# A recurrence phase on one core: tile scores as sums over rows, scores turned by transposes over two banks, fewer keys in a block's first half

## The reference, cut to what matters

```python
def step(state, inp):                       # 8 heads of 64, for each position
    k_t, v_t, w_t, r_t = inp
    kv = k_t[..., :, None] * v_t[..., None, :]
    state = (1.0 - w_t)[..., :, None] * state + kv
    out = jnp.einsum('bhd,bhde->bhe', r_t, state)
    return (state, out)
...
y = outs.transpose(1, 0, 2, 3).reshape(Bv, Tv, Cv) @ Wo.T
...
slope_sign = jnp.sign(jnp.mean(spline_slopes, axis=-1))      # 64 tiles x 8 dims
tile_sigs = tile_sigs.at[jnp.arange(NUM_TILES)[:, None], DIMS].set(slope_sign)
cluster_sigs = jnp.sign(tile_sigs.reshape(NUM_CLUSTERS, TILES_PER_CLUSTER, D).mean(axis=1))
input_sigs = jnp.sign(xf)                                    # xf: the normed rows
cluster_scores = input_sigs @ cluster_sigs.T
best_cluster = jnp.argmax(cluster_scores, axis=-1)
tile_scores = input_sigs @ tile_sigs.T
in_cluster = cluster_assign[None, :] == best_cluster[:, None]
tile_idx = jnp.argmax(jnp.where(in_cluster, tile_scores, -jnp.inf), axis=-1)
```

## Time and profile before

| | |
|---|---|
| median of 3 executions | 8651.39 us (8645.66 to 8653.18) |
| the profiled execution | 8648.8 us, span 8647.0 us |
| core_phase, 7060 to 8430 us: busy PE, DVE, POOL, ACT | 1211.48, 1069.02, 671.15, 357.77 of 1370 us |
| scan_phase, 390 to 5200 us: busy PE, DVE, POOL, ACT | 4345.28, 4543.37, 4439.76, 3671.34 of 4810 us |
| granted TensorE clock, core_phase | 0.87 of full |

### The profile page before, as it was taken

One profiled execution on the slowest core, in us unless ns is written; L12 is line 12 of the kernel. 1 busy time (PEld: TensorE's weight loads), 2 busy tenths in 40 slices (PEclk: granted clock), 3 DMA queues, 4 the chain that ended last, 5 costly groups with the idle time before them and its releaser, 6 DMA issues. The chain is left out here.

```text
span 8647.0 us, 222908 instructions
## 1 busy us (share of the span) xinstructions
PE 7638.4 (88%) x76550; PEld 5615.1 (65%) x76550; DVE 6621.9 (77%) x8318; ACT 4702.7 (54%) x10584; POOL 5670.5 (66%) x3272
## 2 busy tenths in 40 slices
PE   5659999999989989989999999899999989999984
PEld 3337777777777777777777777644444436666653
DVE  4439999999999999999999999622222237878776
ACT  4447777777777777777777787511111112222220
POOL 0009999999999999999999999600000015554544
PEclk8779999999999999999999999999999988988885
DMA  3350000000000000000000000121221222222215
GB/s 134 137 158 0 20 21 0 20 21 1 19 21 20 0 21 20 0 21 20 8 13 20 20 0 5 60 83 68 87 82 68 92 79 78 76 79 74 79 66 168
DMA packets 198786, 423.53 MB, mean 49 GB/s; under 512 B 22448, under 2 KB 48496, under 8 KB 183024
## 3 DMA queue, kind: packets, MB, share of 16 engines
q1 hardware_dynamic: 172768, 382.77, 13.2%
q10 hardware_dynamic: 25872, 38.80, 1.2%
HBM read 225.11 MB, written 196.41 MB: 49 GB/s over the span
## 5 line engine op out<-in xcount | busy, mean ns | idle before, releaser
L485 POOL TENSOR_TENSOR scan_hc<-scan_h,scan_cb 128x1024 f32<-128x1024 f32 x2048 | 4776.9, 2366 | 265.8 <-DMA scan_cb<-scratch_bc 127.5
L651 DVE TENSOR_TENSOR_SCAN scan_h<-scan_a,scan_carry,scan_u 128x512 f32<-128x512 f32 x4096 | 4802.1, 1260 | 156.0 <-PE scan_u L590 128.1
L590 PE MATMUL scan_u<-scan_dg,scan_v 64*128 64x128 f32 x32768 | 2391.7, 286 | 339.1 <-DVE scan_h L651 280.1
L536 ACT ACTIVATE scan_a<-scan_dt,scan_aneg 128x512 f32<-128x512 f32 x4096 | 2659.9, 708 | 44.8 <-issue 30.5
L590 PEld LDWEIGHTS scan_u<-scan_dg,scan_v 64*128 64x128 f32 x32768 | 2000.7, 188 | 819.1 <-DVE scan_h L651 538.0
L598 PE MATMUL scan_y<-scan_ident,scan_hc 128*128 128x128 f32 x16408 | 2251.0, 280 | 60.1 <-POOL scan_hc L485 33.6
L598 PEld LDWEIGHTS scan_y<-scan_ident,scan_hc 128*128 128x128 f32 x16408 | 1764.8, 141 | 310.3 <-POOL scan_hc L485 34.5
L507 ACT ACTIVATE scan_dg<-scan_half,scan_bt 128x64 f32<-128x64 f32 x4096 | 1139.2, 341 | 5.0 <-DVE scan_onward L634 5.0
L528 ACT ACTIVATE scan_carry<-scan_h,scan_onward 128x4 f32 (+1 forms) x1008 | 303.0, 301 | 1042.5 <-DVE scan_h L651 1042.5
L177 POOL TENSOR_TENSOR mid_r<-mid_ve,mid_half_neg 128x4 f32<-128x4 f32 x32 | 32.4, 1012 | 1271.4 <-DVE mid_ve L132 784.1
L1141 POOL TENSOR_TENSOR core_joint<-core_own 128x32 f32<-128x32 f32 x64 | 17.4, 272 | 621.2 <-DVE core_own L1271 536.6
(11 more groups left out here) (211 smaller groups left out, 7647.3 us busy)
## 6 DMA issues: line engine op xcount, KB each, us to landing
scratch_y<-scan_yo ACTq DMA_DIRECT2D x17, 1024.0 KB, 4.7
pre_x<-in_x SPq DMA_DIRECT2D x16, 1024.0 KB, 6.8
scratch_z<-pre_zt SPq DMA_DIRECT2D x16, 1024.0 KB, 3.9
scratch_dt<-pre_dt SPq DMA_DIRECT2D x16, 1024.0 KB, 4.6
scratch_vr<-pre_vr ACTq DMA_DIRECT2D x16, 1024.0 KB, 4.7
scan_dt<-scratch_dt SPq DMA_DIRECT2D x16, 1024.0 KB, 5.3
scan_v<-scratch_vr SPq DMA_DIRECT2D x32, 512.0 KB, 7.8
scan_z<-scratch_z SPq DMA_DIRECT2D x16, 1024.0 KB, 10.7
```

Of the source, the lines that this page charges most:

```text
L485: pool.tensor_tensor(hc[:, q].rearrange("p n (r j) -> p n r j", j=P), h[:, q].rearrange("p n (r j) -> p n r j", j=P), cb[:, bass.ds(b * NS ...
L536: ins = act.activation(a[:, q, n, :], dt[:, par, q, :], ACT.Exp, scale=aneg[:, q, bass.ds(m * 2 + n, 1)])
L590: mm = pe.matmul(u_ps[:, q % 2, g, k * HP:(k + 1) * HP, :], v[row, par, k, q, :], dg[row, buf, k], start=True, stop=True)
L651: ins = dve.tensor_tensor_scan(h[:, q, n, :], a[:, q, n, :], u_ps[:, q % 2, :, :, n].rearrange("p g t -> p (g t)"), carry[:, q, bass.ds(m ...
```

## The change

Three things change in each item, and some constants.

1. Tile scores. `turn_x` and `tile_scores` leave PE. ACT takes the sign of `xf` directly into `sg`. POOL has a new piece, `flip`, that multiplies `sg` by a row of slope signs `sgn`, 128x512, in place. DVE's `route` then sums eight neighbours (128x512 to 128x64), sums eight of those per cluster, and combines both and `key_row` in two `scalar_tensor_tensor` instructions. `route` moves ahead of `spread_scores` in DVE's list, and `flip` stands ahead of `keys` in POOL's.
2. Turned scores. `turn_scores` becomes eight transposes of 128x128 that fill both banks of `sc_ps`; `spread_scores` reads every 16th column.
3. Products. In the first half of a block's positions only the first four keys are multiplied, 256 columns in place of 512, and ACT copies as much; the rest of `scs` is zero from a memset at the start.

The row `sgn` is made once, at the start of the phase: DVE makes four diagonals, PE multiplies them with ones, ACT copies the result; POOL, ACT and PE wait for it.

```diff
-        scores_ps = sc_ps[:, 0, 0:SUB * H].rearrange("p (t h) -> p t h", h=H)
+        turned_ps = sc_ps[:].rearrange("p g (t n) -> p (g t) n", n=P)
+        scores_ps = turned_ps[:, :, 0:P:P // H]
...
+            def flip(i, par, m):
+                act_r.wait(pool, i, 2)
+                pool_b.inc(pool.tensor_tensor(sg[:], sg[:], sgn[:], ALU.mult))
...
-            pipelined(pool, ITEMS, [(1, root), (3, totals), (4, keys), (1, pick), (4, more_keys)])
+            pipelined(pool, ITEMS, [(1, root), (3, totals), (1, flip), (4, keys), (1, pick), (4, more_keys)])
...
-                pe_r.wait(dve, i, 2)
-                dve.tensor_tensor(key[:], sc_ps[:, 1, 0:NT], key_row[:], ALU.add).then_inc(key_read, 1)
-                dve.wait_ge(key_read, i + 4)
+                pool_b.wait(dve, i, 2)
+                dve.tensor_reduce(ts[:], sg[:].rearrange("p (n e) -> p n e", e=8), AX.X, ALU.add).then_inc(key_read, 1)
+                dve.wait_ge(key_read, i + 2)
+                by_cluster = lambda t: t[:].rearrange("p (c n) -> p c n", n=8)
+                after.link(dve, dve.tensor_reduce(cl[:], by_cluster(ts), AX.X, ALU.add))
+                after.link(dve, dve.scalar_tensor_tensor(out=by_cluster(both), in0=cl[:].rearrange("p (c n) -> p c n", n=1).broadcast_to([P, NT // 8, 8]), scalar=512.0, in1=by_cluster(ts), op0=ALU.mult, op1=ALU.add))
+                after.link(dve, dve.scalar_tensor_tensor(out=key[:], in0=both[:], scalar=64.0, in1=key_row[:], op0=ALU.mult, op1=ALU.add))
...
-            pipelined(dve, ITEMS, [(1, state), (1, norms), (0, limits), (1, centred), (4, decays), (3, spread_scores), (1, route)])
+            pipelined(dve, ITEMS, [(1, state), (1, norms), (0, limits), (1, centred), (4, decays), (1, route), (3, spread_scores)])
...
+            act.wait_ge(sgn_made, 1)
+            act.copy(sgn[:], y_ps[:]).then_inc(sgn_ready, 1)
...
-                pe_r.wait(act, i, 1)
-                act_r.inc(act.activation(sgt[:], kt_ps[:], ACT.Sign))
+                after.wait(act, i, S_XF)
+                act.wait_ge(key_read, i + 1)
+                act_r.inc(act.activation(sg[:], xf[:], ACT.Sign))
...
+            for q in range(Q):
+                mm = pe.matmul(y_ps[:, q * P:(q + 1) * P], ones[:], diag[:, q, :], start=True, stop=True)
+            mm.then_inc(sgn_made, 1)
+            pe.wait_ge(sgn_ready, 1)
...
-                pe.wait_ge(key_read, i + 1)
...
-                        mm = pe.matmul(sc_ps[q * 32:(q + 1) * 32, g], heads[:].rearrange("p h n -> p (h n)"), rk[:, par, rows, :, q * NI:(q + 1) * NI].rearrange("p t j i -> p (t j) i"),
+                        mm = pe.matmul(sc_ps[q * 32:(q + 1) * 32, g, 0:SUB // 2 * seen * NI], heads[:].rearrange("p h n -> p (h n)"), rk[:, par, rows, 0:seen, q * NI:(q + 1) * NI],
...
-                    mm = pe.matmul(scores_ps[:, t, :], scs[:, t].rearrange("p i j -> p (i j)"), ident[:, 0:P:P // H], start=True, stop=True)
+                    mm = pe.transpose(turned_ps[:, t, :], scs[:, t].rearrange("p i j -> p (i j)"), ident[:])
...
-            pipelined(pe, ITEMS, [(2, tree), (2, turn_keys), (3, products), (1, turn_x), (2, reads), (3, turn_scores), (1, tile_scores), (2, sums), (2, outputs)])
+            pipelined(pe, ITEMS, [(2, tree), (2, turn_keys), (3, products), (2, reads), (3, turn_scores), (2, sums), (2, outputs)])
```

More of the change, by code:

```diff
@@ L1010, in core_phase @@
         eps_mul = sb("eps_mul", [P, 2]); eps_add = sb("eps_add", [P, 2]); keep = sb("keep", [P, 2])
-        key = sb("key", [P, NT]); kmax = sb("kmax", [P, 1]); pen = sb("pen", [P, NT]); mm2 = sb("mm2", [P, 2])
+        ts = sb("ts", [P, NT]); cl = sb("cl", [P, NT // 8]); both = sb("both", [P, NT]); key = sb("key", [P, NT]); kmax = sb("kmax", [P, 1]); pen = sb("pen", [P, NT]); mm2 = sb("mm2", [P, 2])
         oh = sb("oh", [P, ITEMS, NT]); xs = sb("xs", [P, ITEMS, 8]); ext = sb("ext", [P, 2, NT])
@@ L1043, in core_phase @@
         act_a = Count(sem("act_a"), 4)
-        after = Count(sem("after"), 15)
-        S_STATE, S_X3, S_VE, S_KEEP, S_XF, S_OH = 1, 2, 5, 10, 12, 14
-        pool_b = Count(sem("pool_b"), 2)
+        after = Count(sem("after"), 18)
+        S_STATE, S_X3, S_VE, S_KEEP, S_XF, S_OH = 1, 2, 5, 10, 12, 17
+        pool_b = Count(sem("pool_b"), 3)
         routed = Count(sem("routed"), 5)
-        pe_r = Count(sem("pe_r"), 2)
         act_r = Count(sem("act_r"), 2)
@@ L1126, in _ @@
             pool.wait_ge(pool_ready, 1)
[L1127 removed]
+            pool.wait_ge(zeroed, 11)
+            pool.wait_ge(sgn_ready, 1)
             def root(i, par, m):
@@ L1202, in _ @@
             routed.start(dve)
-            dve.sem_inc(key_read, 3)
-            for t, value in ((kz, 0.0), (rk, 0.0), (s, 0.0), (ext, -BIG), (own, 1.0), (eps_mul, 1.0), (eps_add, EPS)):
+            dve.sem_inc(key_read, 1)
+            for t, value in ((kz, 0.0), (rk, 0.0), (s, 0.0), (scs, 0.0), (ext, -BIG), (own, 1.0), (eps_mul, 1.0), (eps_add, EPS)):
                 dve.memset(t[:], value).then_inc(zeroed, 1)
@@ L1208, in _ @@
             last.then_inc(zeroed, 1)
+            dve.memset(ones[:], 1.0)
             dve.memset(rr[:, SUB - 1, SUB], 1.0).then_inc(zeroed, 1)
-            dve.wait_ge(zeroed, 9)
+            dve.wait_ge(zeroed, 10)
             dve.memset(eps_mul[:, 1:2], 1.0 + EPS)
             dve.memset(eps_add[:, 1:2], EPS * EPS).then_inc(zeroed, 1)
-            dve.wait_ge(zeroed, 10)
-            dve.wait_ge(consts, 144)
+            dve.wait_ge(zeroed, 11)
+            dve.wait_ge(consts, 128)
             dve.tensor_reduce(slope_sign[:], slopes[:], AX.X, ALU.add).then_inc(slope_sum, 1)
@@ L1321, in _ @@
             act.activation(slope_sign[:], slope_sign[:], ACT.Sign, scale=1.0 / GRID).then_inc(slope_signs, 1)
-            act.wait_ge(zeroed, 10)
+            act.wait_ge(zeroed, 11)
+            act.wait_ge(sgn_made, 1)
+            act.copy(sgn[:], y_ps[:]).then_inc(sgn_ready, 1)
             def own_reads(i, par, m):
@@ L1352, in scores @@
                     pe_a.wait(act, i, 1 + g)
-                    moved.inc(act.copy(scs[:, g * (SUB // 2):(g + 1) * (SUB // 2)], sc_ps[:, g].rearrange("p (t j i) -> p t i j", i=NI, j=SUB)))
+                    seen = (g + 1) * (SUB // 2)
+                    moved.inc(act.copy(scs[:, g * (SUB // 2):(g + 1) * (SUB // 2), :, 0:seen], sc_ps[:, g, 0:SUB // 2 * seen * NI].rearrange("p (t j i) -> p t i j", i=NI, j=seen)))
             def kept(i, par, m):
@@ L1375, in _ @@
             pe_b.start(pe)
-            pe_r.start(pe)
-            pe.wait_ge(consts, 144)
-            pe.wait_ge(zeroed, 10)
+            pe.wait_ge(consts, 128)
+            pe.wait_ge(zeroed, 11)
             pe.wait_ge(tiles_ready, 1 + Q)
@@ L1415, in turn_keys @@
                 pool_a.wait(pe, i, A_KEYS)
-                act_r.wait(pe, i - 2, 2)
+                act_a.wait(pe, i - 1, 3)
                 for q in range(Q):
@@ L1428, in products @@
                     for q in range(Q):
-                        rows = slice(g * (SUB // 2), (g + 1) * (SUB // 2))
-                        mm = pe.matmul(sc_ps[q * 32:(q + 1) * 32, g], heads[:].rearrange("p h n -> p (h n)"), rk[:, par, rows, :, q * NI:(q + 1) * NI].rearrange("p t j i -> p (t j) i"),
+                        rows, seen = slice(g * (SUB // 2), (g + 1) * (SUB // 2)), (g + 1) * (SUB // 2)
+                        mm = pe.matmul(sc_ps[q * 32:(q + 1) * 32, g, 0:SUB // 2 * seen * NI], heads[:].rearrange("p h n -> p (h n)"), rk[:, par, rows, 0:seen, q * NI:(q + 1) * NI],
                                        start=True, stop=True, tile_position=(0, q * 32))
                     pe_a.inc(mm)
[L1434 to L1441, removed]
             def reads(i, par, m):
@@ L1666, in program @@
             ln_scale, ln_bias, wx, ww, bw, wk, wv, wr, wo, gamma, beta, slopes, table,
-            ident, half_ident, key_row, key_pattern, sub_mask, head_mask, grid, out):
+            ident, half_ident, key_row, sub_mask, head_mask, grid, out):
     B, L, D = x.shape
```

16 lines of the change are left out of this document (7 added, 9 removed).

## The result

The changed kernel takes 8706.13 us (median of 4 runs, 8703.79 to 8707.03), the kernel before 8650.39 beside it: 1.0065 times as long, with a 95% interval of 1.0047 to 1.0082. That is slower, by 56 us where 36 were forecast. The profiled execution has a span of 8705.2 us, 58.2 more than before's 8647.0.

A forecast was written before the change was run, and what follows sets the result against it. POOL and DVE's loop was taken as the bound: 19.77 + 0.43 + 0.85 = 21.05 us a turn against 20.50, +32 us over 59 turns; +10 start, -6 edges: 8687 us, range 8635 to 8714, its own 8673 to 8701.

The forecast's parts named there:

- The bound: In core_phase's turns, POOL and DVE close the short turn of 19.77 us; PE sets only turns with a low clock.
- the chain of 19.77 us: Short turn before: DVE starts on POOL's root at 10.59 us after own, then centred and decays take 9.18; no PE work.
- The flip: POOL's in-place sign product runs amid DVE's decays on the loop: costs 0.85 us a turn, bounds 0 and 1.3.
- The late `pick`: DVE's two new route instructions are held by POOL's keys, so POOL's pick starts 0.43 us late each turn.
- PE's long turns: Turns such as 23.10 us, where DVE waits for PE's y_ps, were to go: worth 43 us.
- rival D: PE idles more, its clock falls and y_ps is late again: all turns 23.10 us, 8808 us, chance 0.05.
- The signs of being wrong: Turns staying at 19.8 us (no holds), or coming in several lengths again (PE or its clock).
- Rival A: One more DVE instruction is held behind POOL, so DVE closes the turn at 21.4 us: 8708 us, chance 0.12.
- The ends: Outside the 59 turns: start of the phase +10 us for making sgn, end -5, first turns -1.

The follow-up runs named there:

- e7: Kernel before the change, with POOL's root moved ahead of its last two key products: 8653.96 us, ratio 1.0007.
- e8: Kernel before the change, with POOL's root moved ahead of its last two key products and the change's smaller products and scs copy: 8647.37 us, ratio 0.9999.
- e4: Changed kernel with the products and the turning of the scores put back as before, the new sums kept: 8709.94 us, ratio 1.0069.
- e11: Changed kernel with POOL's flip on 256 of the 512 columns alone: 8673.63 us, one execution.
- e1: Changed kernel with POOL's flip left out, signs not multiplied by the slope signs: 8635.69 us, ratio 0.9982.
- e5: Changed kernel with POOL's pick moved behind the joining and widening of the next level: 8679.95 us, ratio 1.0036.
- e3: Changed kernel with the flip moved from POOL to DVE, at the head of route: 8671.99 us, ratio 1.0023.
- e9: Changed kernel with the flip on DVE at the head of route and POOL's pick behind the joins: 8641.64 us, ratio 0.9989.

## Why the prediction came out as it did

The direction, the place and the mechanism were right; two terms of the turn were too small. The 8706 lie inside the range of 8635 to 8714, but outside the 8673 to 8701 that the forecast gave to itself.

*The bound.* Right. POOL and DVE close the turn in every variant but e7 and e8, and the chain of 19.77 us reappears term by term in the 21.42. e4 shows that PE's work in `products` and `turn_scores` was worth next to nothing in a turn of the changed kernel.

*The flip, taken as 0.85 us.* The step that failed is "an in-place product without broadcast can hardly be slower than `pick`". The flip takes 1.26 us at least and 1.33 where it meets DVE; `pick` takes 1.09. The nearer row was L1181, a product of the same size with one operand repeated over the eight positions, which stood beside it at 1.27 and which I had used as the upper bound alone. The 0.2 us that DVE loses less than POOL's length, from the earlier trace rows, was right: 1.33 - 0.24 = 1.09, and e11 repeats it at half the size. The term measured 1.10 on the timeline: 0.25 too little, times 59 = 15 us. By e1 it is 1.17, 0.32 too little or 19 us. The Trainium skill's rule of a whole instruction (SBUF — State Buffer, Who interferes with whom), applied to 1.09, gave nearly the right term for a wrong reason: the whole instruction is 1.33, and the loss is 0.24 less.

*The late `pick`, taken as 0.43 us.* It measured 0.58 (3.27 against 2.69) where the flip came in time, and 0.50 without the flip (e1, `pick` 3.20 after `own` less 2.70). The one-hot came earlier than forecast, 2.89 us after `own` and not 3.08, though `key` was held to 0.77; `both`, reckoned at about 0.5, took 0.38. But `pick` follows its end by 0.28 to 0.38 us and not 0.04. POOL's first joint starts 0.07 us after the end of `own` (7791.29 to 7791.36), so the signal is the smaller part; the rest I take for POOL's own preparation of `pick`, which wasn't tested. That is 0.15 x 59 = 9 us by the timeline, 0.07 x 59 = 4 by e1. The two splits differ, the sum doesn't: 15 + 9 or 19 + 4, for the 23 us that the turns lack. Undoing the wait gave 0.42 back (e5) and not 0.58: `own` to the root is 9.98 there, 0.12 more than before, since the second join now stands right behind the widening that it reads and waits 0.08 for it.

*PE's long turns.* Right: no L1240 waits, and no turn of 23. They are no longer closed by PE although its clock is lower, 0.81 against 0.87 over the phase, with more idle time in between; rival D didn't come.

*The signs of being wrong.* One of them came by its letter: the turns had several lengths again, and not one of 21.0. It wasn't PE or its clock, the causes named with it, but the two places of the flip, which the prediction didn't foresee; it expected one decay longer in every turn, and that came in half of them.

*Rival A* has the nearest time (8708), but not by its mechanism. DVE doesn't close the turn: L1251 still waits 0.60 us for the root. It is a coincidence of sums.

*The ends.* The start was forecast at +10 and came to +9.2, the end at -5 and came to -8.6, the first turns at -1 and came to -1.8. Together with the turns (+32 forecast, +55 measured): 23 too little in the turns, 5 too much at the edges. The parts measured make +54; the medians differ by 55.7, and the two profiled spans by 58.2, with the 4.2 in front of the phase.

*Open.* Why DVE's loss is 0.24 us less than the length of POOL's instruction, and what decides which of the two goes first, wasn't tried. In the changed kernel the two cases lie 0.08 us apart in start: of the 29 long flips among the last 60, 28 start 0.04 us ahead of the next decay step, and the short ones 0.11 or more. But the lead isn't the rule: one that started 0.12 us ahead was shut out too, and in e5 some that started up to 0.30 us ahead of the next step. The 0.08 itself comes from ACT, whose sign starts 0.03 or 0.11 us after the end of `xf`; why, the traces don't show.

## What to carry to other kernels

Work given to an idle engine isn't free when it reads where the engine on the path reads: price it by its own length, from the row with the same operands and size, and ask whether the engine on the path could do it itself for less (here 0.69 for 1.1), and what it will hold in its turn (here 0.35 us of POOL's first joint). A saving on the engine with the highest busy share is worth what the turns that it closes are longer than the next loop, and nothing beyond. When moving one wait away, look for what used to run inside it: that work lands somewhere else, here beside the two longest products of POOL.

## What the runs showed of the hardware that was not expected

A GpSimd instruction that reads SBUF can be shut out by a stream of VectorE instructions with two inputs in SBUF for as long as the stream lasts: 7.30 us for one that takes 1.26, and it shows as busy time of POOL. The source line of the flip:

```profile
L1192 POOL TENSOR_TENSOR core_sg<-core_sg,core_sgn x64: 1262/4740/7383, 7144.2 to 8476.1; 128x512 f32<-128x512 f32 x64
```

POOL's busy time in the phase rose by 277 us (948.07 against 671.15), of which 64 flips at 1.26 us are 81; the rest is time in which the flip waited. The one that is held in the end is the first VectorE instruction that isn't of this kind, a copy of 64 columns with 1.32 for 0.21. The two cases lie 0.08 us apart in the flip's start, and they made the starts of `own` alternate by 2.1 us while POOL's joints came evenly. It goes the other way too: beside DVE's flip (e3, e9) POOL's first joint took 0.62 us in place of 0.27.
